# Block tables of a mixture-of-experts kernel built one block per partition and turned into rows by TensorE

## The chip, the cores and the metric

The kernel runs on one core of one Trainium2 chip. The metric is the device time of one execution in microseconds; lower is better. Beside it stands a profiled execution, whose span (first to last instruction of the core) is a little shorter than its device time.

## What is computed

A cross-attention layer and a mixture-of-experts layer, each added to x through a tanh gate. The first part has 8 batches of 256 rows. The second sends each of the 2,048 rows to two of eight experts.

```python
x = x + jnp.tanh(g_xattn[0]) * xattn(_layernorm(x), ctx_1024, Wq, Wk, Wv, Wo)
x = x + jnp.tanh(g_ffn[0]) * ffn(_layernorm(x), gate_w, gate_up_proj, down_proj)

# ffn: x is (2048, 256), 8 experts, hidden width 1024
probs = jax.nn.softmax(x @ gate_w.T, axis=-1)
w, idx = jax.lax.top_k(probs, 2)
w = w / jnp.sum(w, axis=-1, keepdims=True)
combine = jnp.zeros((T, E)).at[jnp.arange(T)[:, None], idx].add(w)
def step(acc, inputs):
    gup, dn, ce = inputs
    g, u = jnp.split(x @ gup.T, 2, axis=-1)
    return acc + ce[:, None] * (jax.nn.silu(g) * u @ dn.T), None
```

## The kernel before

**Stages.** The attention runs first, one batch after another. While it runs, each row's two experts are picked and ranked, and the list `token_at` is built: 8 experts times 17 columns of 128 places, each place holding the number of a row. After that the expert layer runs over blocks: a block is 128 places of one expert. The 4,096 picks make at least 32 and at most 39 blocks, because each expert's last block may be partly filled. Block s of the loop is done in `step(s, ...)`, which every engine has its own version of.

**Tables.** What block s is isn't known when the program is built, so VectorE works out five rows of 44 whole numbers, the tile `tab`, which the engines' sequencers read with `value_load`: row 0 is the expert of block s, row 1 and row 2 say which of the next expert's weight pieces are to be split during this block, row 3 says whether the block is used, row 4 is its column in `token_at`. All comes from `nblk` (blocks of each expert, 8 numbers), its running sum `endblk`, `startblk` and `skip`. All of these stand alike on all 128 partitions; the tables are made by comparing `endblk` or `startblk` with the 44 block numbers over 44 x 8 = 352 elements and summing over the 8 experts (lines 1360 to 1388). Line 1354 to 1359 make a short table of the first 8 columns only, `first_tab`, ahead of the rest.

**Signals.** Four semaphores tell of the tables: `firsts_ready` (line 1359; GpSimd's first gathers wait for it), `experts_ready` (line 1363; TensorE's step 0), `bases_ready` (line 1369) and `tables_ready` (line 1388; ScalarE's step 0 and GpSimd). VectorE's helper `link` makes an operation and waits until it has ended, so linked operations do not overlap.

**Between the attention and the first block.** TensorE ends the attention's work with `invert` (line 902), issues `stay_warm(3)`, three matmuls of 128x512 in fp32 whose result nobody reads (line 807; each leaves two records in the trace), then `transpose_x(0)` (line 974), waits for `experts_ready`, and starts step 0. GpSimd gathers the 128 rows of block 0 by an indirect DMA (line 523), then those of block 1, 2 and 3; for each one from block 1 on, a column of `token_at` is first copied (line 515). ScalarE scales the gathered rows (`stage`, lines 704 and 706), and after TensorE's transposition it rounds them to the matmul's type (`x_high`, line 711) and VectorE makes the remainder (`x_low`, line 1243).

**One step.** On TensorE, step s is: `expand(s, 0)` (24 matmuls, line 990), the second half of the block before (`transpose_h` line 1000, `contract` line 1010; not in step 0), `transpose_x(s + 1)`, `expand(s, 1)`, `transpose_h(s, 0)`, and `contract(s - 1, 1)` (not in step 0). ScalarE takes the result of an `expand` through SiLU (`gate`, line 718), VectorE multiplies (`product`, line 1395), and only then can `transpose_h` run. In the code of ScalarE, step 0 stands behind `act.wait_ge(tables_ready, 1)` (line 753). On VectorE all of lines 1365 to 1388 stand between `x_low(0, 0)` and its step 0.

Of the kernel before, what the change touches and what calls it, by code (L numbers as in the profile page):

```python
# [29 lines left out]
P = 128  # L30
# [46 lines left out]
FIRSTS = 8  # L77
# [6 lines left out]
def _const_columns():  # L84
    at = 0
    for name, n in (("ident", P), ("kcos", A), ("ksin", A), ("rope", S), ("before", P), ("prio", E),
                    ("base", E), ("limits", E * NT), ("upto_it", E * E), ("blocks", NCOL),
                    ("first", E), ("alone", E), ("second", E), ("place", P), ("begin", BEGINS), ("token", NT),
                    ("filler", 1)):
        CONSTS[name] = (at, at + n)  # L90
        at += n
    return at
# [7 lines left out]
def build_program(nc, x_d, xT_d, ctx_d, kvw_d, wq_d, wo_d, woT_d, gu_d, dn_d, const_d, out_d):  # L100
    rows_d = nc.dram_tensor("rows_scratch", (T + P, XW), F32, kind="Internal").ap()
    ctx = ExitStack()
    with ctx:
# [3 lines left out]
        def sem(name):  # L107
            return ctx.enter_context(nc.semaphore(name))
# [66 lines left out]
        piece_at = sb("piece_at", [P, 2, E])  # L175
        piece_code = sb("piece_code", [P, 2, E])
        tabf = sb("tabf", [P, 4, NCOL])
        tab = sb("tab", [P, 5, NCOL], I32)
        first_tab = sb("first_tab", [P, FIRSTS], I32)
        first_f = sb("first_f", [P, FIRSTS])  # L180
        first_by = sb("first_by", [P, FIRSTS, E])
        last_block = sb("last_block", [P, 1], I32)
        count_area = area[:, 0:E * NT]
        by_block = area[:, E * NT:E * NT + NCOL * E].rearrange("p (s e) -> p s e", e=E)
        by_base = area[:, E * NT + NCOL * E:E * NT + 2 * NCOL * E].rearrange("p (s e) -> p s e", e=E)
        by_piece = area[:, E * NT + 2 * NCOL * E:E * NT + 4 * NCOL * E].rearrange("p (n s e) -> p n s e", n=2, e=E)
# [20 lines left out]
        at = E * NT + 2 * NCOL * E  # L207
        at += 2 * NCOL * E
        from_begin = area[:, at:at + BEGINS]
        assert at + BEGINS <= KC * B * A and PICKS * P <= 2 * NCOL * E  # L210
# [33 lines left out]
        inv_ps = att[:, 0, INV_AT:INV_AT + BEGINS]  # L244
        rank_ps = sc[:, 0, RANK_AT:RANK_AT + 4 * E].rearrange("p (t e) -> p t e", e=E)

        def c(name, n=P):
# [28 lines left out]
        firsts_ready, bases_ready, experts_ready, tables_ready, all_landed = (  # L276
            sem(n) for n in ("firsts_ready", "bases_ready", "experts_ready", "tables_ready", "all_landed"))
# [103 lines left out]
        def _(pool):  # L381
# [130 lines left out]
            def keep_first(s, i):  # L512

                at = pool.value_load(first_tab[0:1, s:s + 1], min_val=0, max_val=SLOTS - 1)
                nc.gpsimd.tensor_copy(index_in[:, i:i + 1], token_at[:, bass.ds(at, 1)]).then_inc(index_kept, 1)

# [46 lines left out]
            pool.wait_ge(firsts_ready, 1)  # L563
            keep_first(1, 1)
            pool.wait_ge(index_kept, 1)
            gather(1, 1, index_in[:, 1:2])
            for s in range(2, RING):
                keep_first(s, s)
# [4 lines left out]
            pool.wait_ge(bases_ready, 1)  # L573
            pool.wait_ge(tables_ready, 1)
            end_pieces(0)
            keep_first(RING, 0)
            pool.wait_ge(index_kept, 5)
            gather(RING, 0, index_in[:, 0:1])
            keep_first(RING + 1, 1)
# [198 lines left out]
        def _(pe):  # L778
# [255 lines left out]
            stay_warm(3)  # L1034
            transpose_x(0)
            pe.wait_ge(experts_ready, 1)
# [24 lines left out]
        def _(dve):  # L1061
# [226 lines left out]
            for t in range(B + 1):  # L1288
# [39 lines left out]
                if t >= 1:  # L1328
# [20 lines left out]
            all_blocks = c("blocks").rearrange("p (s o) -> p s o", o=1).broadcast_to([P, NCOL, E])  # L1349
            for_blocks = lambda ap: ap.rearrange("p (o e) -> p o e", o=1).broadcast_to([P, NCOL, E])  # L1350
            link(V.tensor_scalar(skip[:, :], nblk[:, :], -1.0, float(CAP // P), ALU.mult, ALU.add))
            find_tokens()
            over = lambda ap, n: ap.rearrange("p (o e) -> p o e", o=1).broadcast_to([P, n, E])
            link(V.tensor_tensor(first_by[:, :, :], over(endblk[:, :], FIRSTS),
                                 c("blocks")[:, 0:FIRSTS].rearrange("p (s o) -> p s o", o=1).broadcast_to([P, FIRSTS, E]),
                                 ALU.is_le))
            link(V.tensor_tensor(first_by[:, :, :], first_by[:, :, :], over(skip[:, :], FIRSTS), ALU.mult))
            link(V.tensor_reduce(first_f[:, :], first_by[:, :, :], AX.X, ALU.add))
            V.tensor_tensor(first_tab[:, :], first_f[:, :], c("blocks")[:, 0:FIRSTS], ALU.add).then_inc(firsts_ready, 1)
            link(V.tensor_tensor(by_block, for_blocks(endblk[:, :]), all_blocks, ALU.is_le))  # L1360
            link(V.tensor_reduce(tabf[:, 0, :], by_block, AX.X, ALU.add))
            link(V.tensor_scalar(tab[:, 0, :], tabf[:, 0, :], float(E - 1), None, ALU.min))
            V.tensor_scalar(last_block[:, :], endblk[:, E - 1:E], -1.0, None, ALU.add).then_inc(experts_ready, 1)
            x_low(0, 0)
            link(V.tensor_tensor(by_base, by_block, for_blocks(skip[:, :]), ALU.mult))
            link(V.tensor_reduce(tabf[:, 3, :], by_base, AX.X, ALU.add))
            link(V.tensor_tensor(tabf[:, 3, :], tabf[:, 3, :], c("blocks"), ALU.add))
            link(V.tensor_scalar(tabf[:, 0, :], c("blocks"), endblk[:, E - 1:E], None, ALU.is_lt))
            V.tensor_tensor(tab[:, 4, :], tabf[:, 3, :], tabf[:, 0, :], ALU.mult).then_inc(bases_ready, 1)
            link(V.tensor_copy(tab[:, 3, :], tabf[:, 0, :]))  # L1370
            link(V.tensor_tensor(startblk[:, :], endblk[:, :], nblk[:, :], ALU.subtract))

            link(V.tensor_copy(piece_at[:, 0, :], startblk[:, :]))
            link(V.tensor_scalar(piece_at[:, 1, :], nblk[:, :], 1.0, -float(NCOL), ALU.is_equal, ALU.mult))
            link(V.scalar_tensor_tensor(out=piece_at[:, 1, :], in0=piece_at[:, 1, :], scalar=1.0,
                                        in1=startblk[:, :], op0=ALU.add, op1=ALU.add))
            link(V.scalar_tensor_tensor(out=piece_code[:, 0, :], in0=nblk[:, :], scalar=1.0, in1=c("alone"),
                                        op0=ALU.is_equal, op1=ALU.mult))
            link(V.tensor_tensor(piece_code[:, 0, :], piece_code[:, 0, :], c("first"), ALU.add))
            link(V.tensor_copy(piece_code[:, 1, :], c("second")))  # L1380
            for n in range(2):
                link(V.tensor_tensor(by_piece[:, n, :, :], for_blocks(piece_at[:, n, :]), all_blocks, ALU.is_equal))
                link(V.tensor_tensor(by_piece[:, n, :, :], by_piece[:, n, :, :], for_blocks(piece_code[:, n, :]),
                                     ALU.mult))
            link(V.tensor_reduce(tabf[:, 1:3, :].rearrange("p n s -> p (n s)"),
                                 by_piece.rearrange("p n s e -> p (n s) e"), AX.X, ALU.add))
            link(V.tensor_copy(tab[:, 1, :], tabf[:, 2, :]))
            V.tensor_tensor(tab[:, 2, :], tabf[:, 1, :], tabf[:, 2, :], ALU.add).then_inc(tables_ready, 1)

# [64 lines left out]
def shape_constants():  # L1454

    out = np.zeros((P, NCONST), np.float32)

    def put(name, value):
        a, b = CONSTS[name]
        out[:, a:b] = value  # L1460

    inv = (np.float32(1.0) / np.float32(10000.0) ** (np.arange(0, HD, 2, dtype=np.float32) / np.float32(HD)))
    ang = np.arange(S, dtype=np.float32)[:, None] * inv[None, :].astype(np.float32)
    cos, sin = np.cos(ang).astype(np.float32), np.sin(ang).astype(np.float32)
    row = np.arange(P) % HR
# [12 lines left out]
    put("blocks", np.arange(NCOL)[None, :])  # L1478
# [63 lines left out]
```

## Time and profile before

| | |
|---|---|
| device time, median of 3 runs | 457.68 us (455.27 to 459.23) |
| device time of the profiled execution | 455.51 us |
| its span | 453.7 us |
| TensorE busy, matmul | 407.9 us, 90% |
| VectorE busy | 220.6 us, 49% |
| ScalarE busy | 204.9 us, 45% |
| GpSimd busy | 258.3 us, 57% |
| mean granted clock of TensorE | 0.947 of full speed |

The numbers of the table are from the profile's page. The chain is the line of work that ended last, followed back through what released each step; an engine's busy share alone does not say that it sets the time. A granted clock of 1.00 is 2.4 GHz, one of 0.50 is 1.2 GHz. Times in the rows are microseconds from the span's start.

### The profile page before, as it was taken

What the parts mean: (1) busy time and instruction counts of PE and PEld (TensorE: products, weight loads), DVE (VectorE), ACT (ScalarE), POOL (GpSimd) and SP (SyncE); (2) the same over time, 40 slices, a digit from 0 to 9 for tenths busy, and PEclk for the clock granted to TensorE, in tenths of its full rate; (3) what the DMA queues carried; (4) which work ended last, traced back from release to release, by engine and by line L of the source; (5) the groups of instructions that cost most, each with busy time, mean ns of one, the idle gap of its engine ahead of it and who ended that gap; (6) DMA issues with size and microseconds to landing.
All of it is one profiled execution on the core that took longest, in us unless ns stands there. A gap on an engine that the chain in (4) does not pass through costs nothing.

```text
span 453.7 us, 10877 instructions
## 1 busy us (share of the span) xinstructions
PE 407.9 (90%) x2468; PEld 342.4 (75%) x2469; DVE 220.6 (49%) x589; ACT 204.9 (45%) x453; POOL 258.3 (57%) x257
## 2 busy tenths in 40 slices
PE   7877787666799999999999999999999999999960
PEld 6644464444688888888898888988889888888850
DVE  2566998886334434344443344443444434434330
ACT  2569866221563246336435622563347336433210
POOL 3116879853467239936953972498229936953221
PEclk9999888859699999999999999999999999999975
DMA  8960024821054213531632461146213541112110
GB/s 274 404 249 25 23 97 169 275 73 48 1 175 138 51 24 110 160 102 24 209 117 42 137 192 24 24 116 210 46 24 89 162 122 24 24 24 37 37 28 12
DMA packets 19625, 46.68 MB, mean 103 GB/s; under 512 B 2369, under 2 KB 13761, under 8 KB 16513
## 3 DMA queue, kind: packets, MB, share of 16 engines
q1 hardware_dynamic: 11632, 35.20, 22.4%
q0 software_dynamic: 6720, 9.64, 11.6%
q10 hardware_dynamic: 1248, 1.57, 1.0%
q8 instruction: 9, 0.15, 0.1%
q14 instruction: 16, 0.12, 0.1%
HBM read 37.67 MB, written 9.00 MB: 103 GB/s over the span
## 4 chain that ended last, share of the span: by engine, by line
PE 75%; DVE 9%; DMA 4%; ACT 3%; POOL 3%; issue 3%; POOLq 1%; SPq 0%; DVEq 0%; ACTq 0%
PE att L1010 21%; PE sc L990 20%; PE misc L990 10%; PE qbank L990 10%; PE pT L1000 6%; DMA x<-in_x 2%; POOL dn L472 2%; PE att L974 2%; ACT gu L638 1%; PE att L789 1%; DVE stats L1074 1%; PE sc L827 1%; DMA out<-xT_all,index_out 1%; DVE dn L1201 1%; PE qbank L814 1%
## 5 line engine op out<-in xcount | busy, mean ns | idle before, releaser
L530 POOL DMA_INDIRECT out<-xT_all,index_out x34 | 54.5, 1604 | 111.8 <-DVE xT_all L1421 97.2
L1010 PE MATMUL att<-dn,hT 128*128 x816 | 115.8, 292 | 0.6 <-DVE hT L1399 0.6
L1010 PEld LDWEIGHTS att<-dn,hT 128*128 128x128 f32 x816 | 103.0, 192 | 1.0 <-issue 0.9
L990 PE MATMUL sc<-gu,xT 128*128 x408 | 102.4, 400 | 0.0
L990 PEld LDWEIGHTS sc<-gu,xT 128*128 128x128 f32 x408 | 74.1, 188 | 14.7
L990 PE MATMUL misc<-gu,xT 128*128 x204 | 81.5, 400 | 1.5 <-ACT xT L711 0.9
L990 PE MATMUL qbank<-gu,xT 128*128 x204 | 81.6, 400 | 0.0
L397 POOL TENSOR_TENSOR gu<-wraw,gu 128x2048 f32 x14 | 64.4, 4614 | 12.8 <-ACT gu L627 12.0
L1395 DVE TENSOR_TENSOR xT_all<-xT_all,sc 128x512 f32<-128x512 f32 x34 | 23.4, 688 | 87.6 <-ACT xT_all L718 87.6
L718 ACT ACTIVATE xT_all<-misc 128x512 f32<-128x512 f32 x34 | 20.3, 598 | 81.0 <-PE qbank L990 74.8
L1395 DVE TENSOR_TENSOR xT_all<-xT_all,qbank 128x512 f32<-128x512 f32 x34 | 23.4, 688 | 62.7 <-ACT xT_all L718 62.7
L1399 DVE TENSOR_TENSOR hT<-pT,hT 128x512 fp32r<-128x512 f32 x68 | 46.5, 683 | 2.9 <-issue 2.8
L990 PEld LDWEIGHTS misc<-gu,xT 128*128 128x128 f32 x204 | 39.2, 192 | 9.5 <-issue 2.3
L1000 PE MATMUL pT<-const,xT_all 128*128 128x128 f32 x272 | 41.2, 275 | 4.5 <-DVE xT_all L1395 2.4
L990 PEld LDWEIGHTS qbank<-gu,xT 128*128 128x128 f32 x204 | 39.3, 193 | 7.4
L1000 PEld LDWEIGHTS pT<-const,xT_all 128*128 128x128 f32 x272 | 34.0, 141 | 14.0 <-DVE xT_all L1395 2.8
L523 POOL DMA_INDIRECT xT_all<-rows_scratch,index_in x37 | 36.6, 990 | 13.7 <-issue 10.1
L722 ACT ACTIVATE hT<-pT 128x512 fp32r<-128x512 f32 x68 | 40.3, 592 | 3.7 <-PE pT L1000 3.7
L718 ACT ACTIVATE xT_all<-sc 128x512 f32<-128x512 f32 x34 | 20.2, 594 | 46.8 <-PE sc L990 46.8
L627 ACT ACTIVATE gu<-wraw 128x2048 f32 (+1 forms) x16 | 30.7, 1919 | 11.1 <-PE att L1010 7.4
L397 POOL TENSOR_TENSOR dn<-wraw,dn 128x2048 f32 x7 | 32.3, 4607 | 0.6 <-issue 0.6
L638 ACT ACTIVATE gu<-sc,shift,rs 128x120 f32<-128x120 f32 x64 | 27.9, 460 | 4.2 <-DVE shift L1113 4.1
(169 smaller groups left out, 482.8 us busy)
## 6 DMA issues: line engine op xcount, KB each, us to landing
wraw<-in_gu SPq DMA_DIRECT2D x16, 1024.0 KB, 5.4
wraw<-in_dn SPq DMA_DIRECT2D x8, 1024.0 KB, 5.2
x<-in_x SPq DMA_DIRECT2D x8, 266.0 KB, 11.7
xT_all<-in_xT SPq DMA_DIRECT2D x4, 512.0 KB, 11.3
out<-x SPq DMA_DIRECT2D x8, 256.0 KB, 2.2
rows_scratch<-x SPq DMA_DIRECT2D x3, 532.0 KB, 3.9
xT_all<-rows_scratch,index_in POOLq DMA_INDIRECT x37, 2.9
out<-xT_all,index_out POOLq DMA_INDIRECT x34, 3.9
```

Source lines behind the costliest of these rows:

```text
L397: nc.gpsimd.tensor_tensor(piece_of(where, 1, p), wraw[:, p * PIECE:(p + 1) * PIECE], piece_of(where, 0, p), ALU.subtract).then_inc(w_lo, 1)
L523: nc.gpsimd.indirect_dma_start(out=xg[:, q, :], out_offset=None, in_=rows_d, in_offset=bass.IndirectOffsetOnAxis(ap=index, axis=0)) .then_ ...
L530: nc.gpsimd.indirect_dma_start(out=out_d, out_offset=bass.IndirectOffsetOnAxis(ap=index, axis=0), in_=y[:, r, :], in_offset=None, compute_ ...
L627: nc.scalar.activation(piece_of(where, 0, p), wraw[:, p * PIECE:(p + 1) * PIECE], ACT.Copy).then_inc(w_hi, 1)
L638: ins = nc.scalar.activation(probs[:, b % 2, j, hh, :], score_ps(j, hh), ACT.Exp, bias=shift[:, hh // PAIR, j, hh % PAIR:hh % PAIR + 1], s ...
L718: nc.scalar.activation(silu[:, hf, :], bank[2 * hf][:, :], ACT.Silu).then_inc(silu_made, 1)
L722: nc.scalar.activation(hT[:, hf, 0, :], bank[4 + hf][:, :], ACT.Copy).then_inc(hT_hi, 1)
L990: mm = nc.tensor.matmul(bank[2 * hf + n][:, :], xT[:, par, xp, k, :], gu_part(where, wp, k * 2 * I + col, HALF), start=(k == 0 and xp == 0 ...
L1000: mm = nc.tensor.transpose(bank[4 + hf][:, j * P:(j + 1) * P], h[:, hf, j * P:(j + 1) * P], ident)
L1010: mm = nc.tensor.matmul(bank[6][:, 0:D], hT[:, hf, hp, j * P:(j + 1) * P], dn_part(where, wp, (hf * JH + j) * D, D), start=(hf == 0 and j ...
L1395: V.tensor_tensor(h[:, hf, :], silu[:, hf, :], bank[2 * hf + 1][:, :], ALU.mult).then_inc(h_made, 1)
L1399: V.tensor_tensor(hT[:, hf, 1, :], bank[4 + hf][:, :], hT[:, hf, 0, :], ALU.subtract)\
```

## The change

The constant row of 44 block numbers gives way to two constant columns, `row` (partition p holds p) and `row_above` (p - 1). Every partition now works out the entries of one block, the one of its own number: 15 operations on 8, 32, or 1 elements per partition, of which 5 are linked and 10 (`aside`) only counted. Their results stand in `tab_rows`, 128 partitions by 5. TensorE multiplies each of its five columns with the identity matrix, which lays it out as a row of 44 on partition 0 of the PSUM bank `misc`, and VectorE copies the 220 numbers to `tab` as integers. `first_tab`, the wide work areas and three of the semaphores are gone: all engines wait for `tables_ready`. `stay_warm(3)` is split into one before and one after the five matmuls. GpSimd's first gathers read `tab` row 4.

```diff
@@ gpsimd
             gather(0, 0, token_at[:, 0:1])
-            pool.wait_ge(firsts_ready, 1)
-            keep_first(1, 1)
+            pool.wait_ge(tables_ready, 1)
+            keep_index(index_in, 1, 1)
...
-            pool.wait_ge(bases_ready, 1)
-            pool.wait_ge(tables_ready, 1)
             end_pieces(0)
@@ tensor
             pe.wait_ge(pT_copied, TB * B)
-            stay_warm(3)
+            stay_warm(1)
+            pe.wait_ge(rows_tabled, 1)
+            for k in range(5):
+                mm = nc.tensor.matmul(tab_ps[:, k * NCOL:(k + 1) * NCOL], tab_rows[:, k:k + 1], ident[:, 0:NCOL],
+                                      start=True, stop=True)
+            mm.then_inc(tab_psum, 1)
+            stay_warm(1)
             transpose_x(0)
-            pe.wait_ge(experts_ready, 1)
+            pe.wait_ge(tables_ready, 1)
             step(0, 0, first=True)
@@ vector
             find_tokens()
...
+            def aside(ins):
+
+                n_step[0] += 1
+                ins.then_inc(dve_step, 1)
+
+            aside(V.tensor_scalar(by_row[:, 0, :], endblk[:, :], c("row"), None, ALU.is_le))
+            aside(V.scalar_tensor_tensor(out=by_row[:, 1, :], in0=endblk[:, :], scalar=c("row"), in1=skip[:, :],
+                                         op0=ALU.is_le, op1=ALU.mult))
+            aside(V.tensor_tensor(startblk[:, :], endblk[:, :], nblk[:, :], ALU.subtract))
+            aside(V.scalar_tensor_tensor(out=code_second[:, :], in0=nblk[:, :], scalar=1.0, in1=c("second"),
+                                         op0=ALU.is_gt, op1=ALU.mult))
+            link(V.scalar_tensor_tensor(out=code_first[:, :], in0=nblk[:, :], scalar=1.0, in1=c("alone"),
+                                        op0=ALU.is_equal, op1=ALU.mult))
+            aside(V.tensor_scalar(tab_rows[:, 3:4], endblk[:, E - 1:E], c("row"), None, ALU.is_gt))
+            aside(V.scalar_tensor_tensor(out=by_row[:, 3, :], in0=startblk[:, :], scalar=c("row_above"), in1=code_second[:, :],
+                                         op0=ALU.is_equal, op1=ALU.mult))
+            link(V.tensor_tensor(code_first[:, :], code_first[:, :], c("first"), ALU.add))
+            link(V.scalar_tensor_tensor(out=by_row[:, 2, :], in0=startblk[:, :], scalar=c("row"), in1=code_first[:, :],
+                                        op0=ALU.is_equal, op1=ALU.mult))
+            link(V.tensor_reduce(row_sum[:, :], by_row[:, :, :], AX.X, ALU.add))
+            aside(V.tensor_scalar(tab_rows[:, 0:1], row_sum[:, 0:1], float(E - 1), None, ALU.min))
+            aside(V.scalar_tensor_tensor(out=tab_rows[:, 4:5], in0=row_sum[:, 1:2], scalar=c("row"), in1=tab_rows[:, 3:4],
+                                         op0=ALU.add, op1=ALU.mult))
+            aside(V.tensor_copy(tab_rows[:, 1:2], row_sum[:, 3:4]))
+            aside(V.tensor_scalar(last_block[:, :], endblk[:, E - 1:E], -1.0, None, ALU.add))
+            link(V.tensor_tensor(tab_rows[:, 2:3], row_sum[:, 2:3], row_sum[:, 3:4], ALU.add))
+            dve.sem_inc(rows_tabled, 1)
+            dve.wait_ge(tab_psum, 1)
+            V.tensor_copy(tab[0:1, :, :], tab_ps.rearrange("o (k s) -> o k s", k=5)).then_inc(tables_ready, 1)
             x_low(0, 0)
```

Lines 1354 to 1363 and 1365 to 1388 of the kernel before, and the constants and tiles that only they use, are removed.

## Rows read from the trace of the kernel before

**Rows 1.** The page: the chain that ended last, shares by engine.

```profile
PE 75%; DVE 9%; DMA 4%; ACT 3%; POOL 3%; issue 3%; POOLq 1%; SPq 0%; DVEq 0%; ACTq 0%
```

**Rows 2.** Stretches: busy us (instructions) of each engine, granted clock, DMA share, GB/s.

```profile
98.40:101.80 3.40, 3.30 (x7) 2.02 (x8) 3.06 (x13) 0.00 (x0) 0.30 (x1) 0.50 0.13 44
101.80:106.60 4.80, 2.03 (x6) 0.58 (x4) 1.21 (x5) 1.08 (x3) 3.02 (x7) 1.00 0.21 58
106.60:112.70 6.10, 6.00 (x26) 4.60 (x26) 5.55 (x19) 0.70 (x2) 1.66 (x2) 1.00 0.17 45
112.70:115.00 2.30, 0.00 (x0) 0.00 (x0) 1.57 (x5) 1.30 (x4) 0.00 (x0) 1.00 0.00 0
115.00:116.40 1.40, 0.78 (x4) 0.42 (x4) 1.04 (x3) 1.16 (x4) 0.00 (x0) 0.67 0.00 0
116.40:122.30 5.90, 5.84 (x15) 4.58 (x16) 0.69 (x1) 2.23 (x3) 2.82 (x1) 0.50 0.01 3
125.00:235.00 110.00, 110.00 (x672) 97.02 (x671) 47.42 (x106) 50.80 (x89) 69.98 (x54) 1.00 0.40 114
```

**Rows 3.** Waits between 98 and 122 us: who, for whom, us in total.

```profile
ACT xT_all L718 <- DVE tab L1388: 6.2, 1, 6.2
PE pT L1000 <- DVE xT_all L1395: 2.4, 1, 2.4
```

**Rows 4.** Timeline, VectorE: start us, us, operation; idle before and its releaser.

```profile
100.45 0.22 DVE L1354 TENSOR_TENSOR first_by<-endblk,const 128x64 f32<-128x64 f32 x1
...
108.23 0.20 DVE L1369 TENSOR_TENSOR tab<-tabf 128x44 int32<-128x44 f32 x1
108.35 0.18 DVE L1370 CAST tab<-tabf 128x44 int32<-128x44 f32 x1
108.56 0.17 DVE L1371 TENSOR_TENSOR startblk<-endblk,nblk 128x8 f32<-128x8 f32 x1
108.76 0.17 DVE L1373 COPY piece_at<-startblk 128x8 f32<-128x8 f32 x1
...
110.65 0.52 DVE L1383 TENSOR_TENSOR area<-area,piece_code 128x352 f32<-128x352 f32 x1
111.21 0.52 DVE L1382 TENSOR_TENSOR area<-piece_at,const 128x352 f32<-128x352 f32 x1
```

**Rows 5.** Timeline, TensorE and what stands around it, up to step 1.

```profile
99.39 4.00 PE L807 MATMUL sc<-const 128*128 128x512 f32 x6
...
103.94 0.98 POOL L523 DMA_INDIRECT xT_all<-rows_scratch,index_in  x1 [0.81 <-POOL index_in L515]
...
105.37 0.44 PE L974 MATMUL att<-const,xT_all 128*128 128x128 f32 x2 [1.98 <-ACT xT_all L704]
...
106.67 0.49 PE L990 MATMUL misc<-gu,xT 128*128 x1 [0.86 <-ACT xT L711]
106.80 0.60 ACT L704 ACTIVATE xT_all<-xT_all 128x256 f32<-128x256 f32 x1 [0.57 <-DMA xT_all<-rows_scratch,index_in]
...
113.70 0.60 ACT L718 ACTIVATE xT_all<-misc 128x512 f32<-128x512 f32 x1 [6.20 <-DVE tab L1388]
```

**Rows 6.** The chain in order of time, step 1 (start us, us) at half and full clock.

```profile
121.52 0.43 PE qbank L990
121.94 0.68 PE pT L1000 x4
...
131.43 0.24 PE qbank L990
131.66 0.44 PE pT L1000 x4
```

**Rows 7.** Nearest operations to those added, grouped by line: count, mean ns.

```profile
L1234 DVE TENSOR_TENSOR area<-att,area 128x138 f32<-128x138 f32 x2 | 0.6, 296 | 0.0
L883 PE MATMUL sc<-chosen,ones_bf 128*128 128x24 bf16 x14 | 0.5, 181 | 0.0
L921 PE MATMUL misc<-gc_quad,woT 128*128 128x8 f32 x4 | 0.5, 235 | 0.0
```

More of the change, by code:

```diff
@@ L76 @@
 BY_POOL = 2
-FIRSTS = 8
 WOG_AT = 160
@@ L86, in _const_columns @@
     for name, n in (("ident", P), ("kcos", A), ("ksin", A), ("rope", S), ("before", P), ("prio", E),
-                    ("base", E), ("limits", E * NT), ("upto_it", E * E), ("blocks", NCOL),
+                    ("base", E), ("limits", E * NT), ("upto_it", E * E), ("row", 1), ("row_above", 1),
                     ("first", E), ("alone", E), ("second", E), ("place", P), ("begin", BEGINS), ("token", NT),
@@ L174, in build_program @@
         skip = sb("skip", [P, E])
-        piece_at = sb("piece_at", [P, 2, E])
-        piece_code = sb("piece_code", [P, 2, E])
-        tabf = sb("tabf", [P, 4, NCOL])
+        code_first = sb("code_first", [P, E])
+        code_second = sb("code_second", [P, E])
+        by_row = sb("by_row", [P, 4, E])
+        row_sum = sb("row_sum", [P, 4])
+        tab_rows = sb("tab_rows", [P, 5])
         tab = sb("tab", [P, 5, NCOL], I32)
-        first_tab = sb("first_tab", [P, FIRSTS], I32)
-        first_f = sb("first_f", [P, FIRSTS])
-        first_by = sb("first_by", [P, FIRSTS, E])
         last_block = sb("last_block", [P, 1], I32)
         count_area = area[:, 0:E * NT]
-        by_block = area[:, E * NT:E * NT + NCOL * E].rearrange("p (s e) -> p s e", e=E)
-        by_base = area[:, E * NT + NCOL * E:E * NT + 2 * NCOL * E].rearrange("p (s e) -> p s e", e=E)
-        by_piece = area[:, E * NT + 2 * NCOL * E:E * NT + 4 * NCOL * E].rearrange("p (n s e) -> p n s e", n=2, e=E)
         wraw = sb("wraw", [P, GU + DN])
@@ L206, in build_program @@
         assert at + (DEPTH - 1) * PICKS * P <= 2 * DN
-        at = E * NT + 2 * NCOL * E
-        at += 2 * NCOL * E
+        at = E * NT
         from_begin = area[:, at:at + BEGINS]
-        assert at + BEGINS <= KC * B * A and PICKS * P <= 2 * NCOL * E
+        assert at + BEGINS <= KC * B * A
         late = xT_all[:, :, :].rearrange("p k n -> p (k n)")
@@ L244, in build_program @@
         inv_ps = att[:, 0, INV_AT:INV_AT + BEGINS]
+        tab_ps = misc[0:1, 0:5 * NCOL]
         rank_ps = sc[:, 0, RANK_AT:RANK_AT + 4 * E].rearrange("p (t e) -> p t e", e=E)
@@ L275, in build_program @@
                              "out_init", "zero_out"))
-        firsts_ready, bases_ready, experts_ready, tables_ready, all_landed = (
-            sem(n) for n in ("firsts_ready", "bases_ready", "experts_ready", "tables_ready", "all_landed"))
+        rows_tabled, tab_psum, tables_ready, all_landed = (
+            sem(n) for n in ("rows_tabled", "tab_psum", "tables_ready", "all_landed"))
         loads_ended = sem("loads_ended")
@@ L567, in _ @@
             for s in range(2, RING):
-                keep_first(s, s)
+                keep_index(index_in, s, s)
             nc.gpsimd.tensor_copy(index_out[:, 0:1], token_at[:, 0:1]).then_inc(index_kept, 1)
@@ L572, in _ @@
                 gather(s, s % 2, index_in[:, s:s + 1])
-            pool.wait_ge(bases_ready, 1)
-            pool.wait_ge(tables_ready, 1)
             end_pieces(0)
-            keep_first(RING, 0)
+            keep_index(index_in, RING, 0)
             pool.wait_ge(index_kept, 5)
             gather(RING, 0, index_in[:, 0:1])
-            keep_first(RING + 1, 1)
+            keep_index(index_in, RING + 1, 1)
             pool.wait_ge(zero_out, 16)
@@ L1348, in _ @@
             link(V.tensor_reduce(endblk[:, :], cum, AX.X, ALU.add))
-            all_blocks = c("blocks").rearrange("p (s o) -> p s o", o=1).broadcast_to([P, NCOL, E])
-            for_blocks = lambda ap: ap.rearrange("p (o e) -> p o e", o=1).broadcast_to([P, NCOL, E])
             link(V.tensor_scalar(skip[:, :], nblk[:, :], -1.0, float(CAP // P), ALU.mult, ALU.add))
             find_tokens()
[L1353 to L1362, printed above, removed]
@@ L1363, in _ @@
-            V.tensor_scalar(last_block[:, :], endblk[:, E - 1:E], -1.0, None, ALU.add).then_inc(experts_ready, 1)
-            x_low(0, 0)
[L1365 to L1388, printed above, removed]
+            def aside(ins):
+                n_step[0] += 1
+                ins.then_inc(dve_step, 1)
+            aside(V.tensor_scalar(by_row[:, 0, :], endblk[:, :], c("row"), None, ALU.is_le))
@@ L1477, in shape_constants @@
     put("upto_it", (np.arange(E)[None, :] <= np.arange(E)[:, None]).reshape(1, E * E))
-    put("blocks", np.arange(NCOL)[None, :])
+    put("row", np.arange(P)[:, None])
+    put("row_above", np.arange(P)[:, None] - 1)
     put("place", np.arange(P)[None, :])
```

3 lines of the change are left out of this document (removed).

## The prediction

> **What bounds the kernel now.** I read the page's chain first: TensorE carries 75% of it [rows 1]. The table of stretches shows where that ends. From 125 us on TensorE is busy without a gap at full clock (110.00 of 110.00 us) [rows 2], so the 32 and more steps of the expert layer are TensorE's own work, and nothing that this change touches makes them shorter. Ahead of them lies a ragged stretch. TensorE has 2.03 us of work in 4.80 us before step 0, is busy through step 0 (106.6 to 112.7), does nothing for 2.30 us, and then works at a granted clock of 0.50, that is 1.2 GHz, from about 115.5 to 122.3 [rows 2]. The waits name the cause. ScalarE's first SiLU (L718) sat 6.2 us for VectorE's L1388, the last table operation, and TensorE's `transpose_h(0, 0)` sat 2.4 us for the product behind it [rows 3]. So the late end of the tables costs the kernel twice: a gap in TensorE's work, and a low clock behind the gap.
>
> **The start of the new tables.** `find_tokens` and all ahead of it stay as they are, so the first new operation starts where L1354 did, at 100.45 [rows 4]. Small linked operations start 0.20 us apart (108.56 to 108.76), unlinked ones 0.12 (108.23 to 108.35); a linked one of 352 elements takes 0.56 (110.65 to 111.21) [rows 4]. Five linked ones are 1.0 us. Ten unlinked ones are 1.2 us if all overlap so and 2.0 us if none does; six of the 15 take their scalar from a column, which no small row here prices, so I allow 0 to 0.6 us. That is 2.2 to 3.6 us; I take 2.7, and `rows_tabled` comes at 103.15.
>
> The Trainium skill (VectorE: DVE Perf Modes, "The TRN2 errata") says that a fixed latency stands between VectorE instructions, and advises tiles of at least 512 elements, which speaks against this change. The rows bear out the fixed part (0.17 us for 8 elements against 0.52 for 352) [rows 4]; if every one of the 15 paid it in full, they would take 3.0 us instead of 2.7. What makes the change pay here is that some twenty of the old operations, half of them wide, leave the path.
>
> **The turn into rows.** Five matmuls with a one-column weight leave ten records if they behave as `stay_warm`, three of which leave six [rows 5]. No row has this shape. Below, 14 tiny bf16 ones took 0.5 us, or 0.4 us for ten; above, four records of 8 columns in fp32 took 0.5, or 1.3 us for ten [rows 7]. 44 columns at half clock stand between; I take 0.9 us, end 104.1. The copy of 220 elements out of PSUM on one partition: 138 took 0.30 [rows 7], so 0.3 to 0.5, with the signals `tables_ready` at 104.6. On VectorE only `x_low(0, 0)` is queued behind this wait, and that cannot run before 106.26, where it ran before.
>
> **What TensorE does until step 0.** The old three `stay_warm` ran 4.00 us from 99.39, the clock rising at about 101.8, behind a stretch with 3.30 busy us in 3.40 [rows 2, 5]. Now one of them runs from 99.39. The three took 2.4 us at half clock and 1.6 at full, which would be 5.6 at half clock or 1.9 each, and 1.7 without the drain that each end shows. It ends at 101.1, TensorE idles 2 us, and the second runs from 104.1 to 105.8 still at half clock. So `transpose_x(0)`, which ran at 105.37 [rows 5] when the gathered rows were there, slips 0.4 us and costs about 0.2 more, and step 0 starts at 107.3 in place of 106.67.
>
> **GpSimd.** Its first read of a table moves from `first_tab` to `tables_ready` at 104.6. The gather of block 1 was issued at 103.94, 1 us behind the copy of its column; now I put it at 105.8. From issue to ScalarE's `stage(1)` it was 2.86 us (103.94 to 106.80) [rows 5], so `stage(1)` comes at 108.7. TensorE wants it for `transpose_x(1)` behind `expand(0, 0)`, at 110 at full clock and 112 at half clock. That is the cover: 1 to 3 us. The gathers of blocks 2 and 3 and `end_pieces(0)` have a whole step more. The old wait for `tables_ready` in front of `end_pieces(0)` goes.
>
> **Step 0 and the gap.** A matmul of the `expand` starts every 0.43 us at half clock and every 0.23 at full [rows 6]; in the chain, `expand` of one half is 12 such steps. Step 0's TensorE work, two halves and two transpositions, is 5.75 us at full clock. How much of it is done at half clock is the largest unknown. In one place the clock rose at the end of 3.4 dense us at half clock, in the other at the end of 5.9 [rows 2]. I take 4.5 us from 107.3 at half clock; work of 4.5 us at half clock would have been 2.4 at full, so 2.1 us are lost, and the step ends at 107.3 + 5.75 + 2.1 = 115.1. Now nothing is awaited there: SiLU and product of the first half are done 1.4 us after `expand(0, 0)` ends, at about 113.8, and `transpose_h(0, 0)` follows at once (0.44), then `expand(1, 0)`. The old kernel had 0.6 to 0.9 us between these two; the queue can now run ahead, and I allow 0.2. So 115.8 + 2.75 = 118.5 for the point that the chain had at 121.94, and the transposition there is 0.24 shorter at full clock [rows 6]. The gain is 3.6 us: about 0.7 from the gap and its restart after step 0's own loss is paid, and 2.9 because `expand(1, 0)` and the transpositions around it run at 2.4 instead of 1.2 GHz. Nothing later gives it back, since TensorE's work has no gap [rows 2].
>
> **The sum.** Against the profiled execution: 455.51 - 3.6 = 451.9 us. The median of the runs is 457.68, 2.2 us above that execution, and I do not know which part of the ragged stretch differs between them. The 0.7 us of waiting are sure in each; the 2.9 us of clock may be smaller in executions whose clock rises sooner behind the gap. I take three quarters of them: 2.9 us in all, and **454.8 us** against the median.
>
> **Rivals.** (a) *TensorE is at full clock all through step 0*, because the five matmuls, the filler and the transpositions from 103.2 to 106.3 are enough. For it: the clock stayed at 1.00 over 101.8 to 106.6 with 2.03 busy us [rows 2], so it need not be low once it is up. Against it: it was at 0.50 up to 101.8, and what raised it then, the second and third filler, is gone from there. It saves the 2.1 us: 452.7. (b) *Step 0 runs at half clock to its end, or the tables are a microsecond late*, and what the gap cost is paid ahead of it. 5.75 us of work at half clock cost 5.0 us instead of 2.1: 457.7, no change. For it: 5.84 busy us at half clock stand in one stretch of the trace [rows 2]. The Trainium skill (TensorE: Matmul & The Clock Gate, "What's actually happening") has the low clock as the default, which activity lifts; by that rule two fillers fewer speak for (b), and the trace agrees so far that the clock rose while the fillers ran. (c) *The hand-over becomes the wait.* Step 0 now waits for VectorE, TensorE and VectorE again in turn, and no operation hides it. `tables_ready` has 1.7 us to spare ahead of 106.3; with the 2.9 us gained it decides at 109.2, from where the kernel is slower, one for one. That would take nearly 9 us from 100.45 where I have 4.1, against every row: at 110.2 it gives 458.7, at 114 over 1% slower. (d) *The change does not do what it says*: ScalarE would still wait for the tables at the first SiLU. It would take a table end after 112; the number of operations excludes it.
>
> **How the numbers follow.** My forecast has 0.52, (a) 0.17, (b) 0.24, (c) and (d) 0.07. The likeliest case spans 453.2 to 456.5. The range reaches to (a) with the whole 3.6 us behind it, 451.8, and to (b) with a late table, 458.4. A change of this kernel under 1%, 4.6 us, can hardly be told from none. Faster by over 1% means below 453.1: most of (a) and an eighth of the forecast, 0.23. Slower by over 1% means above 462.3: 0.05. Within 1%: 0.72.
>
> **What would show it.** Right: no wait of L718 for VectorE, `tables_ready`'s copy ending near 104.6, step 0's first matmul near 107.3, no idle TensorE between 113 and 116, a clock of 1.00 from about 112 on. Wrong: TensorE waiting for the copy of `tab`, or for block 1's rows; a clock that falls again in step 1; a step 0 with matmuls 0.43 apart to the end.

## The result

The changed kernel takes 452.95 us in the median of 20 runs (450.14 to 455.88), the kernel before 456.21 us in the median of 20 (453.19 to 459.29). The ratio is 0.9932 with a 95% interval of 0.9912 to 0.9953: faster by 3.1 us (2.1 to 4.0), clear of the noise in its sign and under 1% in size. The forecast was 2.9 us. The ratios leave out the few executions that are over 1.5% above the fastest of their kernel; the medians are of all. The profiled execution has a span of 452.6 us.

The chain by engine, from the page of the changed kernel, has TensorE's share at 81% where it was 75% [rows 1]:

```profile
PE 81%; DVE 9%; DMA 3%; issue 2%; ACT 1%; POOL 1%; POOLq 1%; SPq 0%; DVEq 0%
```

The two profiled executions can't be laid over each other by their times. In the changed kernel's, the attention, which has the same instructions in both, ended 3.07 us later: `token_at` (L1232, before L1238) starts at 103.24 where it started at 100.17. I therefore give times from that operation's start, and call this "from the list". The kernel before, in the lines that the comparison needs (start us, us, operation, idle before and its releaser):

```profile
100.17 0.36 DVE L1238 SCALAR_TENSOR_TENSOR token_at<-area,const 128x136 int32<-128x136 f32 x1
...
113.46 0.20 DVE L1388 TENSOR_TENSOR tab<-tabf 128x44 int32<-128x44 f32 x1
114.33 0.69 DVE L1395 TENSOR_TENSOR xT_all<-xT_all,qbank 128x512 f32<-128x512 f32 x1 [0.66 <-ACT xT_all L718]
115.07 0.78 PE L1000 MATMUL pT<-const,xT_all 128*128 128x128 f32 x4 [2.41 <-DVE xT_all L1395]
...
116.46 0.79 PE L990 MATMUL misc<-gu,xT 128*128 x1 [0.61 <-DVE xT_all L1395]
...
121.74 0.88 PE L1000 MATMUL pT<-const,xT_all 128*128 128x128 f32 x4
```

And the timeline of the changed kernel, from the list to step 1:

```profile
103.24 0.36 DVE L1232 SCALAR_TENSOR_TENSOR token_at<-area,const 128x136 int32<-128x136 f32 x1
103.52 0.23 DVE L1350 TENSOR_SCALAR by_row<-endblk,const 128x8 f32<-128x8 f32 x1
103.65 0.22 DVE L1351 SCALAR_TENSOR_TENSOR by_row<-endblk,const,skip 128x8 f32<-128x8 f32 x1
103.79 0.16 DVE L1353 TENSOR_TENSOR startblk<-endblk,nblk 128x8 f32<-128x8 f32 x1
103.86 0.16 DVE L1354 SCALAR_TENSOR_TENSOR code_second<-nblk,const 128x8 f32<-128x8 f32 x1
...
105.40 0.15 DVE L1370 TENSOR_TENSOR tab_rows<-row_sum 128x1 f32<-128x1 f32 x1
105.66 0.89 PE L1025 MATMUL misc<-const,tab_rows 128*1 128x44 f32 x10 [1.19 <-DVEq L1371]
106.48 2.08 PE L795 MATMUL sc<-const 128*128 128x512 f32 x2
106.59 0.38 DVE L1373 CAST tab<-misc 1x220 int32<-1x220 f32 x1 [1.04 <-PE misc L1025]
...
107.74 0.60 ACT L692 ACTIVATE xT_all<-xT_all 128x256 f32<-128x256 f32 x1 [6.75 <-DMA xT_all<-rows_scratch,token_at]
...
108.40 0.69 PE L962 MATMUL att<-const,xT_all 128*128 128x128 f32 x2
109.85 0.79 PE L978 MATMUL misc<-gu,xT 128*128 x1 [0.77 <-ACT xT L699]
...
114.77 0.60 ACT L706 ACTIVATE xT_all<-misc 128x512 f32<-128x512 f32 x1 [2.31 <-PE qbank L978]
...
117.47 0.60 PE L988 MATMUL pT<-const,xT_all 128*128 128x128 f32 x4
117.83 0.48 PE L978 MATMUL misc<-gu,xT 128*128 x1
...
120.67 0.60 PE L988 MATMUL pT<-const,xT_all 128*128 128x128 f32 x4
```

The fifteen operations take 2.0 us, the five matmuls with their ten records 0.89, the copy 0.38. ScalarE's SiLU (L706) waits for TensorE, no longer for VectorE's tables [rows 3, 5], and the transposition at 117.47 waits for nothing.

The table of stretches, changed kernel (busy us and instructions by engine; granted clock, DMA share, GB/s):

```profile
98.40:101.80 3.40, 1.90 (x8) 1.54 (x8) 3.00 (x12) 1.97 (x4) 1.40 (x5) 0.50 0.44 152
101.80:106.60 4.80, 3.61 (x17) 1.89 (x17) 3.41 (x23) 0.00 (x0) 1.23 (x1) 0.50 0.06 13
106.60:112.70 6.10, 5.33 (x11) 2.97 (x12) 0.79 (x2) 1.78 (x5) 2.56 (x6) 0.50 0.13 40
112.70:115.00 2.30, 2.30 (x11) 1.84 (x10) 0.00 (x0) 0.23 (x1) 0.94 (x1) 0.77 0.32 74
116.40:122.30 5.90, 5.90 (x37) 5.11 (x36) 1.59 (x4) 3.90 (x5) 0.59 (x1) 1.00 0.01 3
125.00:235.00 110.00, 110.00 (x675) 96.98 (x674) 47.31 (x105) 50.11 (x88) 71.89 (x57) 1.00 0.40 114
```

The half clock has moved. It lay in step 1, 116.4 to 122.3 [rows 2]; now it lies in front of step 0 and in its first half, up to about 113.6, and step 1 runs at 1.00. The gap of 2.30 us [rows 2] is gone. Counted from the list, the first half of step 1 ends (its next transposition starts, in the timeline) at 17.43 us (120.67), and it was 21.57 (121.74) before: 4.14 us less. The spans differ by only 1.1 because of the 3.07 lost ahead of it.

### The profile page after: what moved, and what is told of

The parts are those of the page before. It is cut to its first block, busy times and chain, and to the rows that moved or that the text cites. A ratio compares the mean times of both kernels' runs of the same rounds, so it can differ in the third digit from the quotient of the medians.

```text
span 452.6 us, 10881 instructions
## 1 busy us (share of the span) xinstructions
PE 414.0 (91%) x2476; PEld 345.2 (76%) x2477; DVE 213.5 (47%) x577; ACT 204.8 (45%) x453; POOL 257.9 (57%) x257
## 4 chain that ended last, share of the span: by engine, by line
PE 81%; DVE 9%; DMA 3%; issue 2%; ACT 1%; POOL 1%; POOLq 1%; SPq 0%; DVEq 0%
PE sc L978 21%; PE att L998 21%; PE misc L978 11%; PE qbank L978 11%; PE pT L988 6%; DMA x<-in_x 2%; PE att L962 2%; PE att L856 2%; PE sc L815 1%; DVE stats L1068 1%; PE att L777 1%; PE qbank L802 1%; PE misc L832 1%; DVE dn L1195 1%; DMA out<-xT_all,index_out 1%
## 5 line engine op out<-in xcount | busy, mean ns | idle before, releaser
L520 POOL DMA_INDIRECT out<-xT_all,index_out x34 | 54.5, 1604 | 109.3 <-DVE xT_all L1406 101.3
L706 ACT ACTIVATE xT_all<-misc 128x512 f32<-128x512 f32 x34 | 20.3, 596 | 74.2 <-PE qbank L978 74.2
L706 ACT ACTIVATE xT_all<-sc 128x512 f32<-128x512 f32 x34 | 20.2, 593 | 48.6 <-PE sc L978 48.6
```

Of the source, the lines that this page charges most:

```text
L520: nc.gpsimd.indirect_dma_start(out=out_d, out_offset=bass.IndirectOffsetOnAxis(ap=index, axis=0), in_=y[:, r, :], in_offset=None, compute_ ...
L706: nc.scalar.activation(silu[:, hf, :], bank[2 * hf][:, :], ACT.Silu).then_inc(silu_made, 1)
```

## The experiments

Times "from the list" are read in each run's timeline as above: the start of step 0's first matmul, and the end of step 1's first half. The ratio is to the kernel before on the same chip. Rows with the same letter shared a chip and its runs of before. e2, e10 and e11 have 6 executions each, e5 has 9, the other experiments 12, and each has one trace, so where the clock fell is known from one execution of each.

| run | ratio | 95% interval | median us | step 0 starts | step 1's first half ends |
|---|---|---|---|---|---|
| before | 1 | | | 6.50 | 21.57 |
| the changed kernel | 0.9932 | 0.9912 to 0.9953 | 452.95 | 6.61 | 17.43 |
| e1_wide_early, A | 0.9929 | 0.9894 to 0.9963 | 453.81 | 6.58 | 17.20 |
| e2_fill2, A | 0.9863 | 0.9823 to 0.9904 | 449.55 | 6.53 | 15.63 |
| e3_act_wait_late, A | 0.9940 | 0.9908 to 0.9972 | 454.55 | 6.38 | 18.43 |
| e4_dve_busy, A | 0.9940 | 0.9911 to 0.9970 | 453.27 | 6.56 | 18.34 |
| e9_changed_again, B | 0.9904 | 0.9872 to 0.9936 | 451.60 | 6.75 | 17.48 |
| e6_late, B | 0.9942 | 0.9910 to 0.9974 | 453.49 | 8.19 | 18.90 |
| e7_late_no_fill, B | 0.9924 | 0.9890 to 0.9958 | 452.87 | 6.65 | 17.16 |
| e8_fill2_dve_busy, B | 0.9957 | 0.9926 to 0.9988 | 454.23 | 6.46 | 19.82 |
| e11_fill2_again, C | 0.9872 | 0.9824 to 0.9921 | 450.30 | 6.29 | 15.35 |
| e5_no_second_fill, C | 0.9926 | 0.9894 to 0.9957 | 452.52 | 6.55 | 17.69 |
| e10_fill3, C | 0.9891 | 0.9837 to 0.9944 | 450.64 | 6.80 | 16.89 |

**Early tables without TensorE.** The theory is that the tables' end counts, not how they are made.

```diff
@@ kernel before, vector
-            x_low(0, 0)
             link(V.tensor_tensor(by_base, by_block, for_blocks(skip[:, :]), ALU.mult))
...
             link(V.tensor_copy(piece_code[:, 1, :], c("second")))
+            x_low(0, 0)
```

> The kernel before, with the wide tables kept, and x_low(0, 0) moved behind the eight small operations that end with L1380, so that VectorE uses the 3.5 us in which it stood idle (102.8 to 106.3) for table work. My theory (the gain of the change is that the tables end before ScalarE's first SiLU, and that TensorE's gap and the half clock behind it go with that): tables end at about 110.1 on the clock of the profile of before in place of 113.7, 0.2 us after the SiLU could start, so the gap of 2.4 us is nearly gone, all three fillers are kept, step 0 runs at full clock, and the time is 3 to 5 us under before, at or below the changed kernel. Rival (the gain comes from the small operations and TensorE's rows themselves, that is from less work on VectorE or an earlier table for GpSimd's gathers): the time stays within 1 us of before.

Measured: 0.9929, the changed kernel's own ratio, with all the wide operations still there. Timeline of its last table operation and of the SiLU:

```profile
113.16 0.20 DVE L1388 TENSOR_TENSOR tab<-tabf 128x44 int32<-128x44 f32 x1
...
114.48 0.60 ACT L718 ACTIVATE xT_all<-misc 128x512 f32<-128x512 f32 x1 [3.83 <-PE qbank L990]
```

The last table operation starts 9.95 us from the list; before it was 13.29 (L1388 at 113.46). ScalarE no longer waits for them. The rival falls: neither the small operations nor TensorE's rows are needed for the gain, only tables that end before the first SiLU. One part of the expectation failed. The three fillers were kept, and yet the clock, at 1.00 when step 0 began (its first matmul took 0.49 us), was down from about 110.5 to 113.8. TensorE had idled 0.96 us ahead of `transpose_x(0)` and 0.86 behind it; in the kernel before it idled 1.98 and 0.86 there [rows 5] and step 0 ran at 1.00. So the idle time alone doesn't tell when the clock falls, and what brought it down here stays open. TensorE's stretch in this run, with its granted clock:

```profile
110.20:114.00 3.80, 3.80 (x12) 0.55 0.28 72
```

**Which wait it was.** The profile of before names ScalarE's wait, 6.2 us [rows 3].

```diff
@@ kernel before, scalar
-            act.wait_ge(tables_ready, 1)
             step(0, 0, first=True)
...
                 h_high(s, 0)
+                if first:
+                    act.wait_ge(tables_ready, 1)
                 end_pieces(s)
```

> The kernel before with ScalarE's wait for tables_ready moved from in front of step 0 to in front of end_pieces(0), the first place of step 0 that reads a table. The waits of the profile of before name ScalarE as the one who sat for the tables, 6.2 us. My theory: VectorE's own queue is what holds, since product(0, 0) stands behind all table operations, so only the SiLU's 0.6 us leaves the path: 0.3 to 0.9 us under before, and the product starts at about the same 113.7. Rival (it is ScalarE's wait that made the gap): 3 us under before, as the changed kernel.

In the profile the theory holds: the product was expected at about 113.7 on the times of the kernel before and came at 113.56. The first SiLU runs 4 us earlier, and the product still waits for the last table operation:

```profile
113.59 0.60 ACT L718 ACTIVATE xT_all<-misc 128x512 f32<-128x512 f32 x1 [2.09 <-PE qbank L991]
...
117.44 0.20 DVE L1389 TENSOR_TENSOR tab<-tabf 128x44 int32<-128x44 f32 x1
117.56 0.68 DVE L1396 TENSOR_TENSOR xT_all<-xT_all,qbank 128x512 f32<-128x512 f32 x1
...
118.30 0.66 PE L1001 MATMUL pT<-const,xT_all 128*128 128x128 f32 x4 [1.76 <-DVE xT_all L1396]
```

The product starts 13.39 us from the list, 0.77 earlier than before (14.16). But the device time fell by 2.7 us, 1.3 to 4.2 by the interval, where I had 0.3 to 0.9 and the rival 3; by the device time alone the rival would stand, and only the trace speaks against it. The gap before this transposition is 1.76 us instead of 2.41, and in this execution the clock did not fall behind it: 1.00 all through step 1, which alone is 2.4 us of the 3.14 that the stretch is shorter. So the clock is the larger part of what this trace gained, and a gap a little shorter can escape its fall. The mean granted clock of all 12 executions is 0.952, that of the 29 of the kernel before beside them 0.947. My estimate from that: about 4.5 us less at half clock, worth some 2 us, about the part of the 2.7 us that the product's 0.77 leaves. Single executions scatter in their mean clock by more than that difference, and that it is the clock of step 1 in each of them isn't shown.

**The fillers.**

```diff
@@ changed kernel, tensor
-            stay_warm(1)
+            stay_warm(2)
             pe.wait_ge(rows_tabled, 1)
```

> The changed kernel with two fillers in place of one ahead of the five table matmuls (two ahead, one behind). My theory (step 0 of the changed kernel runs its first half at half clock because two of the fillers were taken from in front of it): the clock rises during or before the table matmuls in most executions, the second filler then takes 0.9 us, step 0 starts at full clock, and the time is 1 to 2 us under the changed kernel. Rival (the clock at step 0 is set by something else, or the longer filler delays the table matmuls by what it gains): within 0.5 us of the changed kernel, or above it.

Timeline and stretch of TensorE (the number behind the busy time is the granted clock):

```profile
102.85 0.59 PE L1025 MATMUL misc<-const,tab_rows 128*1 128x44 f32 x10
103.37 1.12 PE L795 MATMUL sc<-const 128*128 128x512 f32 x2
...
106.51 0.49 PE L978 MATMUL misc<-gu,xT 128*128 x1 [0.77 <-ACT xT L699]
...
112.42 0.60 PE L988 MATMUL pT<-const,xT_all 128*128 128x128 f32 x4
```

```profile
104.98:108.98 4.00, 2.91 (x13) 1.00 0.12 34
108.98:113.98 5.00, 5.00 (x26) 1.00 0.19 55
```

Step 0 starts where it did, and now all of it runs at 1.00; its transposition comes 5.91 us after its first matmul, against 7.62 in the changed kernel. Against the kernel before that is 0.9863, and once more, on another chip:

> The changed kernel with two fillers ahead of the table matmuls and one behind, once more, beside the next two on one chip. Expected 0.983 to 0.990 of before, as the first time (0.9863, from 6 runs).

0.9872. One line puts the gain at 5.8 to 6.2 us in place of 3.1 to 4.4 us, and this is the fastest version I have. I had expected 1 to 2 us more; the profiled stretch is shorter by 1.8 and 2.1. The two kernels were not timed on one chip. The intervals of the two fillers (up to 0.9904 and 0.9921) just meet the changed kernel's first (from 0.9912) and overlap its second (from 0.9872), so the device times alone do not settle it; the medians and the profiles point the same way.

More of it does not help:

```diff
-            stay_warm(1)
+            stay_warm(3)
             pe.wait_ge(rows_tabled, 1)
```

> Three fillers ahead of the table matmuls and one behind. At full clock from the third on they end about 0.9 us after rows_tabled, so tables_ready comes 0.9 us later, still ahead of step 0; the clock rises in more executions before step 0. If the clock ahead of step 0 is what counts: within 1 us of the kernel with two ahead. If the filler work in the queue counts as much: step 0 starts 0.5 to 1.5 us later and the time is that much over it.

0.9891: the median is 0.3 us above that of two fillers on the same chip (450.64 against 450.30), within 1 us, as the clock theory had it. The profile is less kind to it: step 0 starts 0.5 us later than in e11, and the stretch is 1.5 us longer, as the rival had it. With 6 executions each the device times can't decide. Most of the rest of the 1.5 us is the next wait. The tables come later, so GpSimd's gather of block 1 does, and at full clock TensorE now waits for it behind step 0's first half:

```profile
111.08 0.44 PE L962 MATMUL att<-const,xT_all 128*128 128x128 f32 x2 [0.86 <-ACT xT_all L692]
```

And the filler behind the matmuls is worth nothing that I could measure:

```diff
             mm.then_inc(tab_psum, 1)
-            stay_warm(1)
             transpose_x(0)
```

> The changed kernel without the filler behind the table matmuls (one ahead, none behind). My theory: at half clock the filler ends just as the rows of block 0 are there, so taking it out moves step 0 no more than 0.2 us ahead, and the clock, which the one filler behind did not raise in the profile, rises no sooner without it: within 1 us of the changed kernel, 0.990 to 0.995 of before. Rival (the filler behind raises the clock in many of the executions): 1 us or more over the changed kernel.

0.9926, and 17.69 us where the changed kernel has 17.43 and 17.48. That is in the range of the theory. The rival, 1 us or more, has little for it: 0.3 us less than the first measurement of the changed kernel, 1.0 more than the second, both on other chips, and 0.2 us more in the profile.

**Work on VectorE that nobody waits for.** The counterpart of the change: early tables, and VectorE's queue full nonetheless.

```diff
@@ changed kernel, vector
             x_low(0, 0)
+            for _ in range(12):
+                link(V.tensor_tensor(area[:, E * NT + BEGINS:E * NT + BEGINS + NCOL * E], const[:, 0:NCOL * E],
+                                     const[:, 0:NCOL * E], ALU.mult))
```

> The changed kernel with 12 linked operations of 352 elements added on VectorE behind x_low(0, 0); nobody reads their result and no semaphore tells of them. They stand for the 7 us of table work that stood there before. My theory: they end some 6.7 us after x_low(0, 0), near 4 us after the first SiLU could be multiplied while step 0 runs at full clock, 2 to 3 us after it at half clock; TensorE's gap before transpose_h(0, 0) comes back and with it the half clock in step 1 in many executions: 1.5 to 4 us over the changed kernel. Rival (the early tables themselves, through the gathers and ScalarE, bring the gain): no more than 0.5 us over the changed kernel.

0.9940 on chip A, against 0.9932 and 0.9904 for the changed kernel on other chips: no difference, or up to 1.6 us, so the device times do not decide between the theory and the rival. The twelve ran 6.68 us, to 115.1, but step 0's first half, partly at half clock, ended only at 113.0 and the second at about 115.9. So `transpose_h(0, 0)` did not wait, the clock stayed at 1.00 in step 1, and the one wait of TensorE that the changed kernel hasn't stands in front of step 1's first matmul:

```profile
PE misc L978 <- DVE xT_all L1383: 0.8, 1, 0.8
```

The stretch is 0.9 us longer. The half clock of step 0 had covered VectorE. So I repeated it with two fillers:

> The changed kernel with two fillers ahead of the table matmuls and with the 12 unread operations of 352 elements on VectorE behind x_low(0, 0). With one filler those 12 cost only about 0.9 us in the profiled stretch, because step 0's first half ran at half clock and so covered part of VectorE's work. My theory: at full clock step 0's first half ends 2 us sooner, so now TensorE waits some 2.5 us before transpose_h(0, 0), and its clock falls in step 1 as in the kernel before: 2.5 to 5 us over the kernel with two fillers alone (449.55), that is 452 to 454.5. Rival (VectorE's queue is not what costs; the fillers are worth 3 us whatever follows): within 1 us of the kernel with two fillers alone.

454.23 us, 0.9957, against 0.9863 and 0.9872 without the twelve operations: 3.9 to 4.3 us lost by the ratios, 4.7 by the first pair of medians, as expected, and 4.2 to 4.5 in the profiled stretch. Its wait and its stretches:

```profile
PE pT L988 <- DVE xT_all L1383: 1.5, 1, 1.5
```

```profile
113.20:114.70 1.50, 0.05 (x2) 0.01 (x1) 1.43 (x4) 0.60 (x1) 0.00 (x0) 1.00 0.00 0
114.70:121.00 6.30, 5.54 (x21) 4.34 (x21) 1.55 (x3) 2.66 (x3) 2.02 (x1) 0.73 0.01 3
```

That is the pattern of the kernel before again: full clock in step 0, then TensorE idle, then a stretch at 0.73. The tables were as early as ever, and nobody reads what was added. What the old tables cost was mainly VectorE's place in the queue in front of the first product.

**How much the hand-over may be late.** The prediction gave `tables_ready` 1.7 us to spare.

```diff
@@ changed kernel, vector
+            for _ in range(3):
+                link(V.tensor_tensor(area[:, E * NT + BEGINS:E * NT + BEGINS + NCOL * E], const[:, 0:NCOL * E],
+                                     const[:, 0:NCOL * E], ALU.mult))
             dve.sem_inc(rows_tabled, 1)
```

> The changed kernel with three linked operations of 352 elements (1.7 us) added on VectorE in front of rows_tabled, so that TensorE's five matmuls, the copy and tables_ready all come 1.7 us later. The prediction held that tables_ready has 1.7 us to spare: by that, no more than 0.3 us over the changed kernel. The other theory, from the trace after (the second filler ends at 108.33 and transpose_x(0) starts at 108.39, with its rows there at 108.34): the filler stands behind the matmuls on TensorE's queue and in front of transpose_x(0), so nothing is to spare, and step 0 starts 1.7 us later, 1 to 1.7 us over the changed kernel.

Step 0 starts 8.19 us from the list where it was 6.75 on the same chip, and the median is 1.9 us higher (453.49 against 451.60; the intervals overlap). TensorE and ScalarE in this run:

```profile
104.32 0.89 PE L1025 MATMUL misc<-const,tab_rows 128*1 128x44 f32 x10 [2.87 <-DVEq L1374]
105.14 2.08 PE L795 MATMUL sc<-const 128*128 128x512 f32 x2
107.01 0.63 PE L962 MATMUL att<-const,xT_all 128*128 128x128 f32 x2
```

```profile
104.63 0.60 ACT L692 ACTIVATE xT_all<-xT_all 128x256 f32<-128x256 f32 x1 [6.65 <-DMA xT_all<-rows_scratch,token_at]
```

The rows of block 0 were scaled at 105.2, and their transposition started at 107.0, behind the filler. The loss is 1.4 us in the profile and 1.7 by the ratios, as the other theory had it. The same delay without the filler:

```diff
@@ added to the edit above, tensor
             mm.then_inc(tab_psum, 1)
-            stay_warm(1)
             transpose_x(0)
```

> The same 1.7 us of delay, with the second filler taken out. If it is the filler in the queue that uses up the time to spare, step 0 starts where it did in the changed kernel or 0.2 us earlier, at half clock as there: within 0.5 us of the changed kernel, and about 1.5 us under the delayed kernel with the filler. If it is the tables themselves that step 0 waits for, both delayed kernels are alike.

Step 0 starts at 6.65 again. The matmuls are as late as before, from 4.10 us from the list, and the transposition follows as soon as its rows are scaled:

```profile
106.77 0.60 ACT L692 ACTIVATE xT_all<-xT_all 128x256 f32<-128x256 f32 x1 [6.62 <-DMA xT_all<-rows_scratch,token_at]
106.49 0.89 PE L1025 MATMUL misc<-const,tab_rows 128*1 128x44 f32 x10 [2.87 <-DVEq L1373]
107.42 0.69 PE L962 MATMUL att<-const,xT_all 128*128 128x128 f32 x2
```

In the profile it is the filler, not the tables, that used up the time. The medians rank the same way (451.60, 452.87, 453.49 for the changed kernel, late without and late with the filler), but not by what I expected: 1.3 us above the changed kernel where I had at most 0.5, and 0.6 below the delayed one where I had 1.5. They are too close for a verdict of their own. The changed kernel on the same chip:

> The changed kernel once more, so that it stands beside the next three on one chip. Expected 0.993 of before, as measured first (interval 0.991 to 0.995).

0.9904, a little better than the 0.991 to 0.995 expected, with the same half clock in step 0 and 17.48 us from the list.

## Why the prediction was right

- **What bounds the kernel.** Right. From 125 us on nothing changed, and e1, e3 and e8 show from three sides that VectorE's table work in front of the first product made the gap. I had named ScalarE's wait of 6.2 us first; by e3's trace it held the product back by only 0.77.
- **The small operations.** I had 2.7 us to `rows_tabled`; from the first operation to the last's end they took 2.0. Unlinked ones start 0.07 us apart (103.79 to 103.86) and 0.13 with a scalar from a column (103.52 to 103.65), so the first kind is below the 0.12 to 0.20 taken from [rows 4] and the second needs nothing of the allowance on top. The Trainium skill (VectorE: DVE Perf Modes, "The TRN2 errata") has its fixed latency between instructions. In these rows a fixed part is in every duration (about 0.15 us even for one element), but operations that do not wait for each other overlap it, and the 3.0 us that I gave beside that page would have been further off. I also wrote that half of some twenty old operations were wide. Of the 20 on lines 1365 to 1388, seven have 352 elements or more.
- **The turn into rows.** 0.9 us predicted, 0.89 measured; the copy 0.38 in 0.3 to 0.5. `tables_ready` came 3.73 us from the list, predicted 4.4.
- **Step 0's start.** Predicted 107.3, that is 7.1 from the list; measured 6.61, before 6.50.
- **Half clock in step 0.** Predicted 4.5 us of it, measured about 3.8 (109.85 to 113.6). This was the largest unknown, and the forecast sat on the right side: rival (a), full clock throughout, did not happen in any profile with one filler ahead; e2 shows that it gives what I said, some 2 us. Rival (b), the whole step, did not happen. With one filler ahead step 0 began at 0.50 in the changed kernel and in e4, e5, e6, e7 and e9; with two or three ahead it began at 1.00 in e2, e8, e10 and e11. The Trainium skill (TensorE: Matmul & The Clock Gate, "What's actually happening") has the low clock as the default, which activity lifts, and these starts agree with it.
- **The restart of step 1.** 1.39 us lay between the transposition and the first matmul before (115.07 to 116.46), 0.36 now. I allowed 0.2 on top of 0.44; there is nothing on top.
- **The sum.** Against the profiled execution I had 3.6 us, of which 0.24 lie in the transposition itself, so 3.4 for the point that came 4.14 sooner. The excess of 0.7 is step 0's start (0.5 sooner than I had it), the shorter half clock (0.7 us less of it is worth 0.3) and the restart (0.3), less some 0.4 of small misses the other way. Against the median I took three quarters of the clock's 2.9 us, 2.9 in all; measured 3.1. That the two are so close is partly luck: the factor of three quarters rests on no row, the interval of the 3.1 is 2.1 to 4.0, and the second measurement (e9) gives 4.4. The time itself, 452.95, is 1.85 below the 454.8 and just below the 453.2 to 456.5 of the likeliest case, mainly since the kernel before has its median at 456.21 over 20 runs where I had 457.68 from three. That the clock's part is not due in every execution is argued rather than shown for the kernel before, of which there is one trace. That a gap may or may not lower the clock is shown: 1.76 us of waiting did not in e3, 1.45 did in e8.
- **Rival (c), where it decides.** Wrong. The 1.7 us to spare counted from `tables_ready` to step 0, but the second filler stands on TensorE's queue between the matmuls and `transpose_x(0)`. `transpose_x(0)` started right behind it at 108.40, just as its rows were there (107.74 and 0.60), so on that path nothing was to spare (e6, e7). The copy of the tables itself, which ended at 106.97, could be later: with 1.7 us of delay and no filler step 0 started as before (e7). The rule of my own that I broke: of a step that is moved, count what is queued behind it.
- **GpSimd's cover.** I had 1 to 3 us. At half clock there was enough. At full clock there is next to none: e2 scaled block 1's rows from 108.71 to 109.3 and TensorE took them at 109.37, and e10 waited 0.86 us.

## What to carry to other kernels

A gap of two microseconds on the engine that sets the time can cost five (here 2.4 of waiting and 2.4 of half clock behind it), because its clock may fall; look at the granted clock after every gap before pricing it. When a profile says that an engine waited for a table, look also at what stands behind the table work on the engine that makes it: using its idle time for table work by moving one operation (e1) gave as much, within the noise, as a new way of making the table. And filler work that raises the clock belongs where it has time of its own: in front of a wait it is free as long as it ends before the wait does (two fillers, not the third of e10), behind one it delays what follows.

## What the hardware did that I had not expected

The same attention instructions took 3.07 us longer to reach the list in one profiled execution than in the other. The change is not the reason: in the second trace of the changed kernel (e9) the list started at 100.94, 2.3 us sooner than in the first. TensorE's granted clock up to 98 us is a difference that the traces show: from 30 to 45 us it was 1.00 in the one and 0.77 in the other.

Kernel before:

```profile
30.00:45.00 15.00, 11.00 (x76) 1.00 0.07 24
0.00:98.00 98.00, 74.13 (x484) 0.90 0.51 181
```

Changed kernel:

```profile
30.00:45.00 15.00, 13.28 (x73) 0.77 0.07 25
0.00:98.00 98.00, 78.94 (x477) 0.84 0.51 178
```

Fewer matmul records (73 against 76) took more of the same 15 us. The 20 runs of the kernel before spread over 6.1 us (453.19 to 459.29), twice what the change is worth, so neither three runs nor the spans of one pair of traces could have shown it. The 20 runs of each did, and the stretch counted from a common operation shows where it lies. Over the 35 runs of the kernel before that stand beside e6 to e9, a lower mean granted clock goes with a longer time (correlation -0.7); why the clock differs from run to run the traces do not show.
